# Row 0's layer-0 weights: block 1 loads beside x, three experts summed by VectorE, tile 0's first low part made by GpSimd

## What is computed

```python
def layer0(x, y, weight, mask, bias):          # weights mixed per row from 8 experts
    w_bot = einsum('bg,got->bot', y, weight * mask)
    return einsum('bnt,bot->bno', x, w_bot) + bias
def layer1(x, onehot, ...):                    # one expert MLP per row, argmax
    hidden = silu(x @ wu.T + bu) * (x @ wg.T + bg)
    return hidden @ wd.T + bd
def layer2(x, router_logits, ...):             # top-2 of 8 gelu MLPs, and a shared one
def layer3(x, w, W_base, b_base, As, Bs):      # base linear and 8 LoRA experts
x = x + layer0(x, cond_8, ...)
x = x + layer1(x, cond_8, ...)
x = x + layer2(x, cond_8, ...)
x = x + layer3(x, cond_8, ...)
```

## Time and profile before

| | us |
|---|---|
| median of 3 runs | 499.66 (499.38 to 500.27) |
| the profiled execution | 499.37 |
| its span | 497.6 |
| TensorE busy | 492.9 (99%) |
| VectorE busy | 343.8 (69%) |
| ScalarE busy | 261.6 (53%) |
| GpSimd busy | 9.7 (2%) |

### The profile page before, as it was taken

The page is one execution under the profiler, slowest core; times in us unless marked ns, Lnnn a source line. Parts: engine busy times, 40 slices in busy tenths (PEclk is TensorE's granted clock), DMA queues, the critical chain, the costliest instruction groups (busy, mean ns, idle before and its releaser), DMA issues.

```text
span 497.6 us, 6556 instructions
## 1 busy us (share of the span) xinstructions
PE 492.9 (99%) x2175; PEld 406.6 (82%) x2175; DVE 343.8 (69%) x602; ACT 261.6 (53%) x416; POOL 9.7 (2%) x14
## 2 busy tenths in 40 slices
PE   8999999999999999999999999999999999999997
PEld 6788788888888888888888888888888888888886
DVE  4858996877778676866766766566575666655645
ACT  5675463566655353555664445455554555444441
POOL 0510000000000000000000000000000000000000
PEclk9999999999999999999999999999999999999999
DMA  8905332332333343233333333232333232331002
GB/s 326 378 38 169 105 95 90 95 97 96 98 97 100 92 133 97 66 97 95 98 101 101 105 114 95 72 103 81 112 95 110 69 124 95 95 97 32 2 0 84
DMA packets 20480, 51.58 MB, mean 104 GB/s; under 512 B 2784, under 2 KB 3552, under 8 KB 20448
## 3 DMA queue, kind: packets, MB, share of 16 engines
q1 hardware_dynamic: 19872, 50.13, 32.2%
q10 hardware_dynamic: 576, 1.05, 0.6%
HBM read 49.07 MB, written 2.10 MB: 103 GB/s over the span
## 4 chain that ended last, share of the span: by engine, by line
PE 98%; DMA 1%; ACTq 0%; issue 0%; DVE 0%
PE act_ps L292 10%; PE act_ps L293 10%; PE act_ps L294 10%; PE lin_ps L293 10%; PE lin_ps L292 10%; PE lin_ps L294 10%; PE acc_ps L292 10%; PE acc_ps L293 10%; PE acc_ps L294 10%; PE aux_ps L292 1%; DMA cols_w<-w_in 1%; PE aux_ps L294 1%; PE aux_ps L293 1%; PE acc_ps L361 1%; ACTq L234 0%
## 5 line engine op out<-in xcount | busy, mean ns | idle before, releaser
L774 DVE TENSOR_TENSOR hid<-lin_ps,act 128x512 f32<-128x512 f32 x96 | 66.4, 692 | 98.0 <-PE lin_ps L294 97.9
L763 DVE TENSOR_TENSOR w_lo<-raw,w_hi 128x384 fp32r<-128x384 f32 (+1 forms) x221 | 122.9, 557 | 0.0
L491 ACT ACTIVATE hid_hi<-hid 128x512 fp32r<-128x512 f32 x112 | 70.8, 632 | 92.0 <-DVE hid L774 77.2
L485 ACT ACTIVATE act<-act_ps 128x512 f32<-128x512 f32 x96 | 57.3, 597 | 115.0 <-PE act_ps L294 115.0
L782 DVE TENSOR_TENSOR hid_lo<-hid,hid_hi 128x512 fp32r<-128x512 f32 x112 | 77.4, 691 | 26.0 <-ACT hid_hi L491 26.0
L471 ACT ACTIVATE w_hi<-raw 128x768 fp32r<-128x768 f32 x111 | 93.0, 838 | 0.0
L292 PE MATMUL act_ps<-x_hi,w_hi 128*128 128x512 f32 x228 | 88.6, 388 | 0.2 <-issue 0.2
L294 PE MATMUL act_ps<-x_hi,w_lo 128*128 128x512 f32 x228 | 88.5, 388 | 0.0
L293 PE MATMUL act_ps<-x_lo,w_hi 128*128 128x512 f32 x228 | 88.5, 388 | 0.0
L292 PE MATMUL lin_ps<-x_hi,w_hi 128*128 128x512 f32 (+1 forms) x226 | 87.7, 388 | 0.0
L294 PE MATMUL lin_ps<-x_hi,w_lo 128*128 128x512 f32 (+1 forms) x226 | 87.7, 388 | 0.0
(11 more groups left out here) (103 smaller groups left out, 327.1 us busy)
## 6 DMA issues: line engine op xcount, KB each, us to landing
raw<-w_in SPq DMA_DIRECT2D x112, 384.0 KB, 3.1
x<-x_in SPq DMA_DIRECT2D x4, 512.0 KB, 6.4
out<-x SPq DMA_DIRECT2D x7, 256.0 KB, 3.6
cols_w<-w_in ACTq DMA_DIRECT2D x4, 256.0 KB, 5.2
cols_w<-w_in SPq DMA_DIRECT2D x2, 256.0 KB, 5.6
cols_w<-w_in SPq DMA_DIRECT2D x1, 288.0 KB, 3.6
mask<-mask_in SPq DMA_DIRECT2D x1, 256.0 KB, 5.3
cols_w<-w_in SPq DMA_DIRECT2D x2, 128.0 KB, 6.7
```

The lines of the kernel that those rows point to most:

```text
L485: act_e.activation(act[:, n % 2, :], act_ps[:, n % 2, :], func, bias=bias).then_inc(act_ready, 1)
L491: act_e.activation(hid_hi[:, n % 2, :], hid[:, n % 2, :], ACT.Copy).then_inc(hid_hi_ready, 1)
L763: ins = dve.tensor_tensor(w_lo[:, n % SPLIT, a:z], raw[:, n % RAW, a:z], w_hi[:, n % SPLIT, a:z].bitcast(F32), ALU.subtract)
L774: ins = dve.tensor_tensor(hid[:, n % 2, :], lin_ps[:, n % 2, :], act[:, n % 2, :], ALU.mult)
```

## The change

SP now issues seven pieces in a row (0, 2, 4, 5, 6, 7, 8). ScalarE issues pieces 1 and 3, the mask, and x of row 0 in two DMAs of 256 KB, one for each feature block, each with a semaphore. TensorE sums five experts of block 0 instead of six and VectorE three instead of two, and TensorE does 16 warm-up matmuls. On ScalarE the priming of Silu comes ahead of the high parts, the first half of tile 0's high part behind block 1's, and the second half of tile 0's behind the new x's second block. GpSimd makes the first half of tile 0's low part, in two instructions of columns 0 to 255 and 256 to 383; its semaphore counts to 2, and tile 1's is a semaphore of its own.

```diff
-PE_EXPERTS = 6
+PE_EXPERTS = 5
-WARMUP = 17
+WARMUP = 16
@@ SP
-            load_w0(sp, 0)
-            load_w0(sp, 2)
-            sp.dma_start(mask[:, :], mask_d).then_inc(mask_in, 16)
-            sp.dma_start(x_row(x_flat, 0), x_d[0]).then_inc(x_in[0], 16)
-            for q in (6, 7, 8):
+            for q in (0, 2, 4, 5, 6, 7, 8):
                 load_w0(sp, q)
@@ TensorE, up_block
                 if n < 2 and c == 0:
-                    pe.wait_ge(w_lo_c0_ready, n + 1)
+                    pe.wait_ge(w_lo_c0_ready[n], 2 - n)
@@ ScalarE
             def split_x0(b):
-                act_e.wait_ge(x_in[b], 16)
+                if b >= 1:
+                    act_e.wait_ge(x_in[b], 16)
                 if b >= 2:
                     act_e.wait_ge(l0_done, (b - 1) * CB)
                 for c in range(CB):
+                    if b == 0:
+                        act_e.wait_ge(x0_in[c], 16)
                     act_e.activation(x_part(x0_hi, b % 2, c), x_part(x_flat, b, c), ACT.Copy).then_inc(x_hi_ready[0], 1)
...
-            for q in (1, 3, 4, 5):
-                load_w0(act_e, q)
+            load_w0(act_e, 1)
+            load_w0(act_e, 3)
+            act_e.dma_start(mask[:, :], mask_d).then_inc(mask_in, 16)
+            for c in range(CB):
+                act_e.dma_start(x_part(x_flat, 0, c), x_d[0, :, c, :]).then_inc(x0_in[c], 16)
...
+            prime(0)
             split_w0(0, 0)
             split_x0(0)
-            prime(0)
+            split_w0(0, 1)
             split_weights0(0)
-            split_w0(0, 1)
-            split_weights0(1)
             split_x1(0)
             split_x1(1)
             split_weights(1)
             split_x(1, 0, 1)
+            split_weights0(1)
             split_weights(2)
@@ VectorE, split_weights
-                if n == 0 and part == 0:
-                    dve.wait_ge(w_hi_c0_ready, 1)
-                else:
-                    dve.wait_ge(w_hi_ready, n + 1)
+                dve.wait_ge(w_hi_ready, n + 1)
...
@@ VectorE, order
             mask_row0(1)
-            split_weights(0, 0)
             split_w0(0, 1)
...
             split_weights(1, 0)
             split_x(1, 0, 1)
+            dve.wait_ge(w_lo_c0_ready[0], 2)
             split_weights(0, 1)
@@ GpSimd, behind the identity
+            pool.wait_ge(w_hi_c0_ready, 1)
+            for a, z in ((0, D), (D, D + P)):
+                pool.tensor_tensor(w_lo[:, 0, a:z], raw[:, 0, a:z], w_hi[:, 0, a:z].bitcast(F32),
+                                   ALU.subtract).then_inc(w_lo_c0_ready[0], 1)
```

More of the change, by code:

```diff
@@ L130, in build @@
         aux_ps = psum("aux_ps", [P, CB, T])
+        x0_in = [sem(f"x0_in{c}") for c in range(CB)]
         x_in = [sem(f"x_in{b}") for b in range(B)]
@@ L166, in build @@
         w_lo_ready = sem("w_lo_ready")
-        w_lo_c0_ready = sem("w_lo_c0_ready")
+        w_lo_c0_ready = [sem(f"w_lo_c0_ready{n}") for n in range(2)]
         act_done = sem("act_done")
@@ L766, in split_weights @@
                     ins.then_inc(w_lo_ready, 1)
-                elif n < 2:
-                    ins.then_inc(w_lo_c0_ready, 1)
+                elif n == 1:
+                    ins.then_inc(w_lo_c0_ready[1], 1)
             def hidden(n, bias):
```

## The result

| | before | after |
|---|---|---|
| median | 499.65 us | 501.26 us |
| lowest and highest | 499.38 to 500.29 | 500.07 to 502.08 |
| the profiled execution | 499.37 | 501.08 |
| its span | 497.6 | 499.0 |
| ratio (95% interval) | | 1.0027 (1.0019 to 1.0034) |

The change makes the kernel slower by 0.27% by the ratio, 1.6 us by the medians. The forecast was +0.2 us, with a range that ended at 500.9. The times after also lie wider: 2.0 us from lowest to highest against 0.9.

What follows compares the result with a forecast made beforehand. TensorE, busy for 99% of the span, bounds the kernel, so only its start-up waits matter. Piece 1's -0.8 and piece 2's +1.0 sum to +0.2: 499.66 + 0.2 = 499.9 us, bounds 499.6 to 500.5, range with rivals 498.9 to 500.9.

Steps and rivals of the forecast that it cites:

- The lost microsecond: Tile 1's first matmul on TensorE starts at S + 5.7 instead of S + 4.77: 1.0 us lost, bounds 0.9 and 1.2.
- Piece 2: Everything behind S up to the tiles: GpSimd's low part hidden, tile 1 held by a semaphore count, 1.0 us lost.
- the count of 2: Finished high parts on ScalarE: tile 1 waits for two, the second now tile 0's half behind x's second block, S + 5.0.
- S: End of TensorE's block 1 sum in the start-up: 12.03 before, forecast 11.2 after.
- GpSimd's own new work: Tile 0's first low part in two GpSimd instructions: 1.1 to 2.3 us together, ending S + 2.5 to S + 3.7, hidden.
- The gain: Piece 1, the start-up up to S: block 1's sum ends at 11.2, 0.8 us gained, bounds 0.4 and 0.9.
- the third piece of block 1: Weight DMA landing at 9.2 to 9.6, with 2.0 us of instructions behind it, so S at 11.2 to 11.6.
- Piece 1 gives nothing: Rival: block 1 stays held by DMA as before, so no gain in S: +1.0, 500.7 us, chance 0.10.
- The second piece: Block 1's second weight DMA, fourth in SP's queue, landing about 8.2 instead of 9.13 by an equal share of the engines.
- to the end undiminished: Stages behind the start-up are one unbroken row of matmuls, so the +0.2 us reaches the end: span 497.8.
- The late clock: Rival: TensorE's clock rises only behind block 0, which ends 2.0 later: +0.2 + 2.0, 501.9 us, chance 0.10.
- Hiding the priming of Silu: ScalarE's priming, 1.28 + 0.20, runs ahead of block 0's rounding, about 7.1 to 8.6: hidden, with little to spare.

Runs made afterwards that it cites:

- experiment 2: The changed kernel repeated as it is, for a second trace and spread: 501.02 us, 1.0026 of before.
- experiment 3: The changed kernel with 20 warm-up matmuls instead of 16: 501.22 us, 1.0029 of before.
- experiment 7: The changed kernel with x of row 0 in one DMA, tile 0's half left where the change put it: 500.37 us, 1.0011 of before.
- the ten traces: Traces with the new load order, seven with x in halves and three with x in one piece; block 1's third piece landed between 9.52 and 10.20.
- the seven traces: Traces with the new load order and x in halves; third piece landed between 9.65 and 10.20, by and large later the deeper the rate dip.
- experiment 5: The changed kernel with tile 0's second half back in its old place and x of row 0 in one DMA: 499.47 us, 0.9985 of before.
- experiment 1: The changed kernel with tile 0's second half back right behind the first on ScalarE: 499.71 us, 1.0005 of before.
- experiment 6: The kernel before with x of row 0 in two half-row DMAs on SP's queue, nothing else: 500.02 us, 0.9999 of before.
- experiment 8: Waits added to TensorE's program: 64 on experiment 1's kernel 499.81 us, 64 on the change 500.9, 128 on experiment 5's 499.34, 68 on before 500.48.
- the 128 waits: Experiment 5's kernel plus 128 waits on already set semaphores, 64 in the warm-up and 64 in down products: 499.34 us, 0.9989 of before.

## Why the prediction was wrong

**The lost microsecond was right.** Piece 2 said that the count of 2 would hold tile 1 until S + 5.7, at a price of 1.0, bounds 0.9 and 1.2. It was S + 5.92 and 1.15. The difference to my value is VectorE's low part, 0.72 in place of 0.55, the upper bound taken from the earlier trace rows: GpSimd was scaling LoRA weights at that moment. Here the Trainium skill (GPSIMD Engine Reference, "Key points"), by which GpSimd and such VectorE instructions contend, and the trace agree. But it isn't always VectorE that pays. In experiments 2, 3 and 7 GpSimd was scaling too, the same instruction took 0.56 and tile 1 came at S + 5.75, while a scaling of GpSimd's right behind took 1.50 to 1.81 in place of 0.92. I had used the rule on the wrong pair. GpSimd's own new work, which I priced with it, took 1.16 for both, as the row of 0.74 had said, and stayed hidden by 0.7.

**The gain was wrong.** The step that failed is S = 11.2. It rested on the third piece of block 1 landing at 9.2 to 9.6, of which I took the early end, with before's own landing called "the upper end", since fewer bytes stood ahead of it. It landed at 10.20, and S was 12.24. Two things were wrong in this. First, I counted the bytes of SP's queue alone. With what ScalarE's queue has to move beside it, 2592 KB have to be moved by the time this piece lands, before (1568 and 1024, ScalarE's queue being empty at 9.13) and after alike (1312 and 1280, if the two have equal shares). So nothing in the bytes brings it sooner than 9.55. The Trainium skill (DMA: Bandwidth & Descriptors, "Issuing engines are not separate DMA queues") has the queues on the same engines; I cited it, took from it that no byte comes sooner, and didn't apply it to this piece. It is 0.4 of the 1.0 by which S was off, and the ten traces agree: none has the piece clearly sooner than 9.55. Second, I took the rate as given. It depended on how x was cut: 262 GB/s instead of 416 in the stretch where the first half of x begins. I had passed over the cut (one DMA of 4 KB rows becomes two of 2 KB rows) in the diff. From 9.55 to 10.20 is the other 0.6; that most of it comes from the dip rests on the estimate above and on the order of the seven traces, and experiment 7, late without a dip, stays open. "Piece 1 gives nothing", at 0.10 and 500.7, was the nearest rival: it had block 1 held by DMA, as it was, but not held longer than before.

**A second term was mis-sized.** The second piece was to land at 8.2, by an equal share of the engines from 6.9 on. It landed at 8.89, since the piece ahead of it landed at 7.52 and not at 6.9, and without the dip, in experiment 5, at 8.82, since x whole took two thirds of the rate. So S is 11.73 there and the gain 0.3, not 0.8.

**The sum** of the profiled executions: +0.21 + 1.15 = +1.4, forecast -0.8 + 1.0. All of the difference but 0.15 is in S. The medians stand 1.6 apart and the two profiled executions 1.4 by their spans.

**What no step had** is the end of the kernel. I said that the shift goes "to the end undiminished". It does, but with a longer tail in part of the executions, when an instruction fetch meets the last stores. The trace before has none there, so nothing in its rows of the start-up could say so; that the next fetch, 21 to 34 us behind the one at 465.8, was due between 487 and 500 could have been read.

**The late clock** occurs, and its price was wrong. In experiments 1, 3 and 6 and in three kernels of experiment 8 the first two to five real matmuls were each followed by the next 0.37 to 0.56 later, in place of 0.22, and in none did it cost the 2.0 us that I gave it: block 0 becomes slower and TensorE then finds the pieces of block 1 landed. With more warm-up nothing was won. Hiding the priming of Silu ahead of the rounding was right, and is worth more than I gave it when block 0 is late: with the old order, in experiment 6, the table load ran from 11.03 to 12.31 and tile 1 came at 17.13, 0.3 later than before.

The version that beats both kernels is the change with the half of tile 0 in its old place and x in one DMA: 0.9985 of before, and 0.9989 with the 128 waits on a third chip. Both intervals only just exclude 1. Of what the change does it keeps the new order of the pieces, the three experts on VectorE, the earlier table load and GpSimd's low part.

## What to carry to other kernels

A wait on a count is a wait on the order of the engine that counts: when a step is moved past another that raises the same semaphore, look for whoever waits for the second count, even if the diff doesn't name it. When a transfer is moved to another queue, count the bytes of both queues up to each landing, and check its shape too; here a DMA that was cut into strided halves for an earlier start slowed everything beside it for a microsecond. And where a change is worth a microsecond, look at the end of the trace too, since a fetch of instructions that drifts into the last stores is as large as the gain.

## What the runs showed of the hardware

- x of 512 KB in rows of 4 KB beside weights in rows of 2 KB: 410 to 424 GB/s between 7 and 8 us. The same x in two DMAs of 2 KB out of every 4 KB: 262 to 385. The busy share of the DMA engines was 1.02 to 1.05 and 0.95 to 1.05. Only the start of the first half is slow; the second half ran at 380 in the change.
- Two queues that are both busy moved like numbers of packets, so the one with rows of 4 KB moved twice the bytes of the one with rows of 2 KB (0.29 and 0.13 MB between 7 and 8 us in experiment 5).
- A fetch of 16 KB of instructions took 0.9 to 2.4 us and came every 28 us in the mean (21 to 34, trace before); with instructions added to TensorE's program it came sooner (482 to 494 us in place of 494 to 500). Among the last stores it raised the landing of the last two from 2.0 to 2.8 us (experiments 2 and 5).
- 68 waits on a semaphore that is already set, four behind each of 17 warm-up matmuls, stretched the warm-up from 3.81 to 4.15 us. The kernel before was 0.14% slower with them (0.05 to 0.23), with a fetch of instructions among its stores.
